# Adding the two parts of dt by accumulating DMAs in place of GpSimd, with z's gates one step later and the expert rows asked for one tile earlier

## The reference, cut to what matters

```python
xz = x @ in_proj_w.T
xp, z = jnp.split(xz, 2, axis=-1)
xc = jax.nn.silu(xc)                      # after a causal convolution of 4 taps over xp
x_dbl = xc @ x_proj_w.T
dt = jax.nn.softplus(x_dbl[..., :dt_rank] @ dt_proj_w.T + dt_proj_b)
...
def step(h, ts):
    dt_t, B_t, C_t, u_t = ts
    dA = jnp.exp(dt_t[..., None] * A)
    h = h * dA + (dt_t * u_t)[..., None] * B_t[:, None, :]
    y = jnp.einsum('bds,bs->bd', h, C_t)
    return (h, y)
...
y = y * jax.nn.silu(z)
return y @ out_proj_w.T
```

## Time and profile before

| what | value |
|---|---|
| time, median of 3 runs | 1527.77 us (1526.65 to 1530.67) |
| profiled execution | 1529.59 us, span 1527.8 us |
| VectorE busy | 1241.7 us, 81% |
| TensorE busy | 1257.8 us, 82% |
| GpSimd busy | 1202.9 us, 79% |
| ScalarE busy | 897.9 us, 59% |

### The profile page before, as it was taken

How to read it: one execution, slowest core, us unless ns; L and a number is a source line. 1 busy time by engine, 2 the same in 40 slices (tenths; PEclk the granted TensorE clock), 3 DMA queues, 4 the chain that set the end, 5 groups by cost and what they waited for, 6 DMA issues and landing times.

```text
span 1527.8 us, 17205 instructions
## 1 busy us (share of the span) xinstructions
PE 1257.8 (82%) x4966; PEld 915.4 (60%) x4966; DVE 1241.7 (81%) x1547; ACT 897.9 (59%) x1972; POOL 1202.9 (79%) x638
## 2 busy tenths in 40 slices
PE   3875473689879988979898997989898998889977
PEld 2642121577667756767676766766686676655546
DVE  6599875599878987798888997799889897977844
ACT  4542453476757756675767765676767475645432
POOL 0444888798898878897799889797999799986830
PEclk8586887799999989999999999999999999979989
DMA  4773543688597757876597758786789569456640
GB/s 170 252 286 132 158 159 117 234 247 251 153 317 227 229 149 223 281 226 224 160 310 237 238 153 275 251 247 194 225 300 271 191 190 326 150 194 204 216 133 28
DMA packets 131518, 325.79 MB, mean 213 GB/s; under 512 B 15176, under 2 KB 29904, under 8 KB 120928
## 3 DMA queue, kind: packets, MB, share of 16 engines
q1 hardware_dynamic: 112224, 272.91, 52.8%
q0 software_dynamic: 13056, 41.95, 11.9%
q10 hardware_dynamic: 6144, 9.83, 1.8%
HBM read 259.75 MB, written 39.71 MB: 196 GB/s over the span
## 4 chain that ended last, share of the span: by engine, by line
PE 42%; DVE 13%; issue 10%; DMA 8%; POOL 8%; ACT 7%; SPq 1%; DVEq 0%; ACTq 0%; POOLq 0%
PE prod L1030 37%; DVE state L1415 9%; DMA xs<-slot_x 7%; POOL slot_x L732 4%; POOL dbu L745 3%; PE prod L1035 2%; ACT state L832 1%; PE prod L1217 1%; DVE prod L1453 1%; PE prod L1218 1%; DVE hxc L1383 1%; DVE late L1480 1%; POOL late L803 1%; PE prod L1082 1%; ACT late L996 1%
## 5 line engine op out<-in xcount | busy, mean ns | idle before, releaser
L1415 DVE TENSOR_TENSOR_SCAN state<-state,carry,dbu 128x512 f32<-128x512 f32 x512 | 657.3, 1284 | 126.3 <-ACT state L832 87.2
L745 POOL TENSOR_TENSOR dbu<-dtu,bb 128x1024 f32<-128x1024 f32 x256 | 630.5, 2468 | 58.3 <-DVE state L1415 50.5
L756 POOL TENSOR_TENSOR hxc<-hxc 128x1024 f32<-128x1024 f32 x155 | 376.9, 2432 | 117.7 <-DVE hxc L1383 117.6
L1383 DVE TENSOR_TENSOR hxc<-state,cb 128x512 f32<-128x512 f32 x512 | 353.6, 691 | 38.9 <-DVE state L1415 1.9
L832 ACT ACTIVATE state<-dt,par 128x512 f32<-128x512 f32 x512 | 352.6, 692 | 52.9 <-DVE hxc L1383 38.0
L1030 PE MATMUL prod<-xsT,late 128*128 128x256 f32 (+1 forms) x1280 | 269.9, 366 | 23.2 <-issue 9.9
L1030 PE MATMUL prod<-late 128*128 128x256 f32 x1136 | 274.2, 399 | 13.2 <-issue 11.7
L1030 PEld LDWEIGHTS prod<-xsT,late 128*128 128x128 f32 x1280 | 226.4, 196 | 70.1 <-issue 31.9
L1030 PEld LDWEIGHTS prod<-late 128*128 128x128 f32 x1136 | 231.9, 207 | 50.6 <-issue 21.9
L1082 PE MATMUL prod<-hxc,ident 128*128 128x512 f32 x212 | 122.2, 708 | 63.6 <-DVE hxc L1383 57.2
L830 ACT COPY carry<-state 128x1 f32<-128x1 f32 x384 | 60.9, 158 | 162.3 <-DVE hxc L1383 154.3
(11 more groups left out here) (168 smaller groups left out, 1254.2 us busy)
## 6 DMA issues: line engine op xcount, KB each, us to landing
bb<-bc_rows SPq DMA_DIRECT2D x256, 256.0 KB, 5.8
cb<-bc_rows SPq DMA_DIRECT2D x256, 256.0 KB, 4.9
late<-moe SPq DMA_DIRECT2D x40, 1028.0 KB, 5.3
late<-moe SPq DMA_DIRECT2D x40, 1024.0 KB, 6.5
hxc<-hxc POOLq DMA_DIRECT2D x36, 512.0 KB, 7.2
slot_x<-xc SPq DMA_DIRECT2D x18, 512.0 KB, 5.8
xs<-slot_x SPq DMA_DIRECT2D x31, 256.0 KB, 6.7
slot_y<-ys ACTq DMA_DIRECT2D x31, 256.0 KB, 5.3
```

Source lines behind the costliest of these rows:

```text
L745: nc.gpsimd.tensor_tensor(dbu[:, v % 3, :, :], dtu[:, n % 2, 2 * h:2 * h + 2, :], b, ALU.mult).then_inc(dbu_ready, 1)
L756: nc.gpsimd.tensor_tensor(hxc[:, to, :, :], hxc[:, to, :, :], hxc[:, piece, :, :], ALU.add).then_inc(summed, 1)
L1383: nc.vector.tensor_tensor(hxc[:, buf, c, :], state[:, k % STATES, :], cb[:, v % 4, :], ALU.mult).then_inc(hc_ready, 1)
L1415: nc.vector.tensor_tensor_scan(state[:, k % STATES, :], state[:, k % STATES, :], dbu[:, v % 3, c, :], carry[:, n % 2, col(k):col(k) + 1], ...
```

## The change

The sum of the two parts of dt is made, for all blocks but the first, by a DMA that GpSimd issues with `accum_op=ALU.add` (14 of them, 512 KB each); the semaphores `dt_sum` tell of its landing, and `dt_formed` waits for them, on GpSimd before DTU and on ScalarE before a half's first decay. DTU0 is two steps later. On VectorE the four gates of z are one step later than before. SyncE asks for the rows of tile i+2 at MT of tile i, ahead of the load of w1 for tile i+1, instead of at NEXT of tile i.

```diff
-           "SPE": 51, "SPL": 52, "DTA0": 53, "DTU0": 55, "DTA1": 64, "DTU1": 68}
+           "SPE": 51, "SPL": 52, "DTA0": 53, "DTU0": 57, "DTA1": 64, "DTU1": 68}
...
-LATER = {"act": {"R": 1, "M": 1, "C": 1, "A": 2}, "dve": {"M": 1, "C": 1, "A": 0}, "pool": {"Y": 1, "A": 1},
+LATER = {"act": {"R": 1, "M": 1, "C": 1, "A": 2}, "dve": {"M": 1, "C": 1, "A": 0, "Z0": 2, "Z1": 2, "Z2": 2, "Z3": 2}, "pool": {"Y": 1, "A": 1},
          "pe": {"Y": 4}, "sp": {"M": 2}}
...
+        dt_sum = [sem("dt_sum0"), sem("dt_sum1")]
...
+        def dt_formed(eng, n, q):
+
+            if n:
+                eng.wait_ge(dt_sum[q], 16 * n)
+            else:
+                eng.wait_ge(dt_ready, q + 1)
...
                     if name == "MT" and i < TILES - 1:
+                        if i < TILES - 2:
+                            if i:
+                                full(sp, ("M", "MT", i - 1))
+                            else:
+                                full(sp, ("M", "START", 1))
+                            load_rows(i + 2)
                         read_out(sp, ("M", "UP%d" % (2 * size(i) - 1), i))
                         load_first(i + 1)
                     elif name == "NEXT" and i < TILES - 1:
                         full(sp, ("M", "DN0", i))
                         load_second(i + 1)
-                        if i < TILES - 2:
-                            load_rows(i + 2)
...
-                    nc.gpsimd.tensor_tensor(half, half,
-                                            dtu[:, p, 2 * q:2 * q + 2, :], ALU.add).then_inc(dt_ready, 1)
+                    if i:
+                        pool.dma_start(flat3(half), flat3(dtu[:, p, 2 * q:2 * q + 2, :]), accum_op=ALU.add).then_inc(dt_sum[q], 16)
+                    else:
+                        nc.gpsimd.tensor_tensor(half, half,
+                                                dtu[:, p, 2 * q:2 * q + 2, :], ALU.add).then_inc(dt_ready, 1)
                 elif kind == "A" and name[:3] == "DTU":
                     p, q = i % 2, int(name[3])
-                    pool.wait_ge(dt_ready, 2 * i + q + 1)
+                    dt_formed(pool, i, q)
...
                 if k % 32 == 0:
-                    act.wait_ge(dt_ready, 2 * n + h + 1)
+                    dt_formed(act, n, h)
```

## The result

The changed kernel takes 1521.2 us (median of 20 runs) against 1530.5 us for the kernel before (20 runs): a ratio of 0.994, 95% interval [0.992, 0.996], 9 us faster. The forecast was 23 us.

What follows compares the result with a forecast made beforehand. No engine was taken as the bound: time is lost where one strict list waits for another. Terms -16 + 3 - 11 - 7 + 6 + 2 = -23 us from 1529.6 gave 1506.6, put at 1506; range 1488 to 1530.

Steps and rivals of the forecast that it cites:

- Gates a step later: VectorE's z gates: next scan and product fill the wait for the tanh, 16 us gained, 3 us lost at OUT0.
- the +3 us: TensorE at OUT0 would stand for the later last z gate: 4 of 8 blocks at 0.75 us each.
- Rows a tile earlier: SyncE's loads for the experts' tiles: TensorE's 55.8 us wait for rows goes, a wait for w2 follows; 11 us gained.
- The reason given for the small gain: TensorE in the experts' tiles: w2 lands only 0.6 us ahead of the rows and its issue does not move.
- dt by DMA: GpSimd's 14 sums become accumulating DMAs: 7 us of relief, against 6 us at DTU1 and 2 us for traffic.
- The added traffic: The 14 DMAs' load on the DMA engines: 32 us of DMA time, priced at 2 us lost.
- The 7 us of relief: GpSimd issues a DMA instead of summing: half the DTAs gain 1.5 us each, 10 us, of which 7 taken.
- The 6 us for DTU1: GpSimd waits 4 to 6 us for DTA1's landing in up to 6 blocks; 1 us a block taken as lost.
- Rival B: GpSimd stalls at DTU1, second accumulation landing late behind the linking DMA where DMA engines are full: slower, 1542 us; chance 0.14.
- the 107 us of the rows in the chain: The DMA bringing the experts' rows, 7% of the chain that ended last, called more than any wait of compute.

## Why the prediction was wrong

**Gates a step later** was right in mechanism and near in size: the wait fell from 37.4 to 4.7 us, -16 + 3 us were forecast and the part alone measured -17 us. OUT0 did not suffer: where TensorE waited 8.1 us for the gates before, it waited 4.4 us after, so the +3 us was not there.

**Rows a tile earlier** was right in its mechanism too: w2 stood directly behind the rows, the wait moved to it, and the part alone gave -7 us where -11 us were forecast. The reason given for the small gain is only half right. That w2 lands just ahead of the rows is in the trace, but removing most of the wait for w2 gave 4 us, so in the kernel without the sums by DMA that wait was largely slack. In the whole change it was not everywhere: the 6.00 us at 1241.57 reach VectorE. Together the two parts gave 25 to 29 us, against 24 us forecast.

**dt by DMA** is the step that failed, and in it the term for what the new DMAs do to the other transfers: "The added traffic, 14 x 2.3 = 32 us of DMA time or 2% of the span, costs nothing at 0.60 and something where the engines are full; I take 2 us." The amount was right (39 us). The price was not: the whole part was costed at -7 + 6 + 2 = +1 us and measures 0.994 to 0.996 against 0.981 to 0.984, 15 to 22 us in the presence of the other two, and 29 us alone. The runs put in its place: transfers that meet in the boundary stretch. The loss shrinks by half or more when DTA1 leaves that stretch, and by 14 us when an unrelated load does, which alone gives nothing. DMAs that nothing waits for bring 17 us of loss at these steps, of which 8 to 12 us are their issue, and none that can be told at steps 38 and 44. The bytes alone thus have 5 us, with overlapping intervals, and no run adds the whole 15 to 22 us up from its parts. The rows had shown the stretch at a DMA share of 1.02, and I priced the newcomer's own landing there, but not that of the loads beside it, on which TensorE, then ScalarE's list, then the decays hang. I also left out what a faster GpSimd sets off: at the boundary before half 14 its linking DMA moves up to 1.2 us behind the second weights. And I left out the clock, which makes TensorE's two late starts in half 14 cost 2.9 and 2.1 us more than the waits themselves. The 7 us of relief is seen only where the halves are 1.2 to 1.6 us shorter; VectorE's wait for forms fell from 38.4 to 35.9 us.

**The 6 us for DTU1**, the term I watched most, was a true wait (17.4 us in 6 places) with no price. The lead of the forms covered it. Rival B named one of the right places and the wrong mechanism: not the stalled GpSimd, but late weights of the experts.

One reading of the prediction is off, without a term that rests on it: the 107 us of the rows in the chain are called more than any wait of compute, but in the kernel before ScalarE waited 154.3 us and GpSimd 117.6 us for VectorE's products.

What stays open: how the 15 to 22 us divide between the bytes, the shifted linking DMA and the clock, and which boundary is hit (12 and 14 here, not 8 or 10). Half 14 stays long with DTA1 moved (90.0 us) although half or more of the loss is back, and with LOADN later it gains only 1.5 us on the repeat of the whole change, so most of what both regain lies elsewhere, in places that were not read. The split between GpSimd's issue and the bytes was measured only with GpSimd's sums still in place, and its intervals overlap.

**The better version** is the change without the sums by DMA: 1499.4 us and 1500.2 us in two measurements, 0.984 and 0.981, with DTU0 two steps later 1499.3 us, 0.982. With LOADN moved as well it is no faster.

A rule of the Trainium skill (page "DMA: Bandwidth & Descriptors", section "Anatomy of one DMA — SWDGE (gpsimd) path") gives an estimate of 3.2 us for such a DMA; the 14 took 4.5 to 13.3 us, 8.0 in the median, so the trace disagrees: even the fastest took longer. The Trainium skill, same page, section "Queues, rings and completion order", says that each DMA engine takes turns between the queues that have work for it; the first weights that took 12.7 us beside GpSimd's two DMAs, instead of 8.9 us beside one, fit with that but do not prove it.

## What to carry to other kernels

A DMA that relieves a busy engine can be paid for by the other loads of the same microseconds: look at the DMA share of the stretch, and ask what the loads beside it are waited for by, and what stands in that engine's list behind them. Ask too which later transfers the relieved engine now starts earlier, and beside what. The newcomer's own landing time can be hidden perfectly and the change still lose. Check the place before the amount: the same bytes 15 to 20 steps earlier cost nothing that could be told. And when a change has several parts, time each alone before keeping them together; here one of three took back more than half of what the others gave.

## What the runs showed of the hardware

GpSimd's operations look longer in the profile behind a DMA that it issued. In the kernel before, behind the linking DMA at 446.84, in its timeline:

```profile
447.43 2.65 POOL L777 TENSOR_TENSOR dt<-dt,dtu 128x1024 f32<-128x1024 f32 x1
449.75 2.64 POOL L745 TENSOR_TENSOR dbu<-dtu,bb 128x1024 f32<-128x1024 f32 x1
452.08 2.60 POOL L756 TENSOR_TENSOR hxc<-hxc 128x1024 f32<-128x1024 f32 x1
```

They last 2.65 us by their records but start 2.32 us apart, so the work goes on at the same rate as elsewhere, and the recorded durations overstate it: with 14 DMAs of 1 KB more, the mean of a form rose from 2.46 to 2.60 us. The distance of the starts is the number to trust.

TensorE's granted clock was 0.50 for at least 4.4 and 3.6 us after waits of 6.00 and 7.18 us, and 1.00 after waits of 2.41 and 1.08 us at the same two places of the other kernel. A late load was thus paid for twice: 32 products took 10.02 and 9.27 us instead of 7.15 and 7.14 us.
